# Finding the first batch's attention maxima inside the experts' blocks, on one set of banks

## What is computed

```
x = x + L0_attn_a(layernorm(x))   # 16 heads of 64, softmax
x = x + L0_ffn(layernorm(x))      # 8 experts, each takes the 64 best of 256 tokens
x = x + L0_attn_b(layernorm(x))   # causal, 16 heads of 8, slope bias m * (k - q)
x = x + L0_ffn(layernorm(x))      # the same experts again
x = x + L1_attn_a(layernorm(x))   # causal, 16 heads of 8, rotated q and k
...
```

```
top_p, top_idx = jax.lax.top_k(probs_et, cap)
h = gelu(einsum('BElC,ECH->BElH', xin, w1))
y = einsum('BElH,EHC->BElC', h, w2) * top_p[..., None]
out = zeros.at[b_idx, top_idx].add(y)
```

## Time and profile before

| | us |
|---|---|
| median of 3 runs | 2353.46 |
| the runs | 2351.25 to 2359.56 |
| the profiled execution, its time | 2350.0 |
| its span, first to last instruction | 2348.3 |
| busy in the span: TensorE, VectorE | 2052.1, 1544.7 |
| busy in the span: ScalarE, POOL | 1199.0, 825.0 |
| mean granted clock of TensorE | 0.932 of full |

### The profile page before, as it was taken

The page is one execution under the profiler, slowest core; times in us unless marked ns, Lnnn a source line. Parts: engine busy times, 40 slices in busy tenths (PEclk is TensorE's granted clock), DMA queues, the critical chain, the costliest instruction groups (busy, mean ns, idle before and its releaser), DMA issues. The chain is left out here.

```text
span 2348.3 us, 52692 instructions
## 1 busy us (share of the span) xinstructions
PE 2052.1 (87%) x20735; PEld 1381.5 (59%) x20735; DVE 1544.7 (66%) x2742; ACT 1199.0 (51%) x2044; POOL 825.0 (35%) x1272
## 2 busy tenths in 40 slices
PE   6999999999959997998689989997599985479996
PEld 3666666666648995555578966664345543335553
DVE  5777777777743435666354447774688875768884
ACT  3444444444343324665623326655477776447774
POOL 4444444444423432332144414441233322433330
PEclk9999999999969998999789989998699997769998
DMA  5000000000000022444000214441244420134441
GB/s 167 1 1 1 1 1 1 1 1 1 1 6 2 14 46 70 113 113 99 2 4 1 55 29 113 113 112 32 70 100 115 113 61 1 42 80 107 113 109 46
DMA packets 142787, 120.97 MB, mean 52 GB/s; under 512 B 11808, under 2 KB 127408, under 8 KB 142548
## 3 DMA queue, kind: packets, MB, share of 16 engines
q1 hardware_dynamic: 142548, 117.64, 21.1%
HBM read 63.48 MB, written 54.12 MB: 50 GB/s over the span
## 5 line engine op out<-in xcount | busy, mean ns | idle before, releaser
L906 DVE TENSOR_REDUCE l_group_mx<-maxima 128x4 f32<-128x1024 f32 x248 | 304.0, 1226 | 69.0 <-PE maxima L699 67.5
L834 ACT ACTIVATE l_group_pr<-scores 128x1024 f32<-128x1024 f32 x256 | 261.5, 1021 | 71.7 <-PE scores L720 69.1
L2171 POOL TENSOR_TENSOR l_wide_tiles_sum<-l_wide_pr 128x256 f32<-128x256 f32 x256 | 180.7, 727 | 212.4 <-ACT l_wide_pr L2114 212.4
L2142 DVE RECIPROCAL l_wide_rc<-bank 128x256 f32<-128x256 f32 x128 | 223.8, 1749 | 8.4 <-PE bank L2075 7.9
L2114 ACT ACTIVATE l_wide_pr<-scores 128x512 f32<-128x512 f32 x256 | 139.1, 595 | 163.1 <-PE scores L2058 163.1
L2126 DVE TENSOR_REDUCE l_wide_mx<-maxima 128x2 f32<-128x512 f32 x248 | 159.4, 685 | 52.6 <-PE maxima L2038 52.0
L906 DVE TENSOR_REDUCE l_slope_mx<-maxima 128x6 f32<-128x768 f32 x124 | 118.9, 959 | 74.2 <-PE maxima L706 72.7
L2104 ACT ACTIVATE l_wide_qk<-bank 128x512 f32<-128x512 f32 x128 | 76.4, 597 | 175.2 <-PE bank L2025 175.2
L906 DVE TENSOR_REDUCE l_rope_mx<-maxima 128x6 f32<-128x768 f32 x124 | 118.8, 958 | 56.3 <-PE maxima L706 55.4
L834 ACT ACTIVATE l_slope_pr<-scores 128x768 f32<-128x768 f32 x128 | 103.5, 809 | 87.0 <-PE scores L727 86.8
L834 ACT ACTIVATE l_rope_pr<-scores 128x768 f32<-128x768 f32 x128 | 103.7, 811 | 77.0 <-PE scores L727 76.8
(11 more groups left out here) (468 smaller groups left out, 4853.5 us busy)
## 6 DMA issues: line engine op xcount, KB each, us to landing
l_group_st<-stack_dram SPq DMA_DIRECT2D x64, 384.0 KB, 5.5
l_slope_st<-stack_dram SPq DMA_DIRECT2D x32, 384.0 KB, 5.6
l_rope_st<-stack_dram SPq DMA_DIRECT2D x32, 384.0 KB, 5.5
stack_dram<-l_group_parts SPq DMA_DIRECT2D x64, 192.0 KB, 2.3
stack_dram<-l_group_parts SPq DMA_DIRECT2D x64, 128.0 KB, 1.9
stack_dram<-l_slope_parts SPq DMA_DIRECT2D x32, 192.0 KB, 2.4
stack_dram<-l_rope_parts SPq DMA_DIRECT2D x32, 192.0 KB, 2.3
stack_dram<-l_slope_parts SPq DMA_DIRECT2D x32, 128.0 KB, 2.3
```

What stands on the lines that cost most here:

```text
L834: act.activation(pr[:, i % AHEAD, :, 0:keys], Tp[:, :, 0:keys], ACT.Exp).then_inc(s["exps"], 1)
L906: dve.tensor_reduce(mx[:, b % 2, :, :, i], max_bank(i, b)[:, :, 0:BLOCKS * keys].rearrange("p z (a k) -> p z a k", k=keys), AX.X, ALU.max, ...
L2142: own.done(dve.reciprocal(rc[:], Ob[i % 2][:, S:2 * S]))
L2171: pool.tensor_tensor(tiles_sum[:, i % 2, z, :], pr[:, i % 2, z, 0:S], pr[:, i % 2, z, S:2 * S], ALU.add).then_inc(s["added"], 1)
```

## The change

For slope and rope the list `FIRST` gets all the work on the first batch's maxima: 8 max, turnmax, join, split, shift and spread. The table of hosts gets slots for them in steps 6 and 7 and `expert_schedule` offers "host" there. In the block these maxima go to the scatter's two banks, now one tensor called `values`; each waits for the reduction of the one before. Turnmax goes to the same banks. In the attention itself the maxima 1 and 3 of batch 1 now alternate to `Tp`, which no score uses yet. The tiles `mx`, `mrest`, `cols` and `rows` are allocated earlier.

```diff
+for _kind in ("slope", "rope"):
+    FIRST[_kind]["pe"] += [("max", _i, 0) for _i in range(PAIRS)] + [("turnmax", 0, 0)]
+    FIRST[_kind]["dve"] += [("max", _i, 0) for _i in range(PAIRS)] + [("join", 0, 0), ("turnmax", 0, 0)]
+    FIRST[_kind]["pool"] += [("split", 0, 0)]
+    FIRST[_kind]["sp"] += [("shift", 0, 0), ("spread", 0, 0)]
...
+for _kind in EXPERT_HOST:
+    for _at in [(6, _slot) for _slot in range(3, 9)] + [(7, 3), (7, 4), (7, 8)]:
+        EXPERT_HOST[_kind]["pe"][_at] = "first"
+    for _at in [(6, _slot) for _slot in range(4, 9)] + [(7, 0), (7, 4), (7, 5), (7, 6), (7, 8)]:
+        EXPERT_HOST[_kind]["dve"][_at] = "first"
+    EXPERT_HOST[_kind]["pool"][7, 6] = "first"
...
         def max_bank(i, b):
-            return Tp if b == 0 and i % 2 else Sp
+            if causal and b == 0:
+                return K.Op
+            return Tp if takes_turns(i, b) else Sp
+
+        def takes_turns(i, b):
+
+            return i in (1, 3) and b == 1 if causal else i % 2 and b == 0
+
+        def settled(i, b):
+
+            turns = (b == 1 and 1 <= i <= 4) if causal else b == 0
+            return PAIRS * b + i - (1 if turns else 0)
...
-                wait(pe, s["maxed"], PAIRS * b + i - (1 if b == 0 else 0))
+                wait(pe, s["maxed"], settled(i, b))
...
                     if b == 0:
-                        pe.wait_ge(s["maxed"], PAIRS)
+                        pe.wait_ge(s["maxed"], PAIRS + 4 if causal else PAIRS)
...
-            done = [fill[what, b] for what, i, b in firsts("pe")[:len(firsts("pe")) - len(todo["pe"])]]
+            done = firsts("pe")[:len(firsts("pe")) - len(todo["pe"])]
+            wait(pe, s["maxed"], sum(1 for what, i, b in done if what == "max"))
+            done = [fill[what, b] for what, i, b in done if what != "max"]
...
-        if 2 <= n <= 5:
+        if 2 <= n <= 7:
             pieces.append(("host", slot))
...
-            following.first("sp", sp, 4 * HOSTED)
+            following.first("sp", sp, 4 * HOSTED + 2)
```

More of the change, by code:

```diff
@@ L438 @@
 }
-FIRST["group"] = FIRST["slope"]
+FIRST["group"] = {_engine: list(_pieces) for _engine, _pieces in FIRST["slope"].items()}
 for _kind in FIRST:
@@ L513, in narrow_attention @@
         va = K.va
-        mx = mrest = cols = rows = pr = rc = ot = att = att_t = None
+        pr = rc = ot = att = att_t = None
+        mx = sb("mx", [P, 2, 2, BLOCKS, PAIRS])
+        mrest = sb("mrest", [P, 2, NT, PAIRS])
+        cols = sb("cols", [P, 2, NT, 3, 2, PAIRS], BF16)
+        rows = sb("rows", [48, 2, S], BF16)
         first_norm = sb("first_norm", [P, 6, HOSTED * NT])
@@ L549, in bank_of @@
         def bank_of(what, b):
-            early = causal and b < HOSTED and what in ("norm", "qk", "swapped", "v")
+            early = causal and (b < HOSTED and what in ("norm", "qk", "swapped", "v") or b == 0 and what == "turnmax")
             return (Ob if early else Mb)[fill[what, b][0]]
@@ L1101, in run @@
         def run():
-            nonlocal mx, mrest, cols, rows, pr, rc, ot, att, att_t
+            nonlocal pr, rc, ot, att, att_t
             assert not any(todo.values())
[L1104 to L1107, removed]
             pr = sb("pr", [P, AHEAD, 2, 2 * S])
@@ L2209, in program @@
         banks = [K.Sp[:, 0, :], K.Sp[:, 1, :], K.Tp[:, 0, :], K.Tp[:, 1, :]]
-        banks += [ctx.enter_context(nc.psum_tensor(f"bank{n}", [P, 512], F32)) for n in range(4, 8)]
+        K.Op = ctx.enter_context(nc.psum_tensor("values", [P, 2, 512], F32))
+        banks += [K.Op[:, 0, :], K.Op[:, 1, :]]
+        banks += [ctx.enter_context(nc.psum_tensor(f"bank{n}", [P, 512], F32)) for n in range(6, 8)]
         K.rows_dram = nc.dram_tensor("rows_dram", [16, S], BF16).ap()
```

## The result

The changed kernel takes 2378.28 us (median of 4 runs, 2369.06 to 2385.48), the kernel before 2352.36 beside it; the ratio is 1.0097, 95% interval 1.0074 to 1.012. In a second comparison it took 2379.65 (6 runs) against 2352.4 (29 runs), ratio 1.0117 (1.0087 to 1.0147). So the change costs 25 to 27 us. Forecast were 2364.8, range 2356 to 2373: the direction was right, but of the loss less than half was foreseen (11.3 us).

What follows compares the result with a forecast made beforehand. TensorE was taken to bound the experts' blocks, the stack's transfer loop the attention's pace. Cost 2 x 11.6 = 23.2 us, less gains 7.2 + 4.7 = 11.9, gave +11.3, hence 2364.8 us; range 2356 to 2373.

Steps and rivals of the forecast that it cites:

- the gain at the start: Attention start: earlier first scores, limited by batch 2's stack, save 7.2 us in slope and 4.7 in rope, 11.9 together.
- The waits: Experts' units 6 and 7: TensorE's maxima wait for VectorE's reductions, three times 0.95 and three times 1.85, 8.4 us per block.
- The free case: Rival for the experts' blocks: VectorE is ready in time, no waits; net -5.5 us, 2348; chance 0.10.
- the halved waits: Rival for the experts' blocks: sooner reductions or overlapping work about halve the waits; net +3 us, 2356; chance 0.12.
- Cost 1: Experts' blocks, TensorE: eight maxima's matmuls at 0.38 us each add 3.0 us per block.
- Cost 3: Experts' last unit: maxima's transposes fit the 0.78 us gap before the last scatter; only their copy costs, 0.2 us per block.
- The waits cost the clock: Rival for the experts' blocks: 1.85 us waits lower TensorE's clock, up to 10 us in all, 2375; chance 0.14.
- the prediction's own sign of being wrong: Experts' blocks: a granted clock below 1.0 there was listed among the observations that would show the forecast wrong.
- the next bound: Attention start: batch 2's stack is late next; just in time in slope, a 1.6 to 2.6 us wait in rope.
- The scale: Whole kernel: the profiled execution was 3.5 us below the median, so 2361.3 on the profile's scale became 2364.8.
- the first rival: Experts' blocks: interleaving is free, no waits; net -5.5 us, 2348; chance 0.10.

Runs made afterwards that it cites:

- the filled waits: Changed kernel, with TensorE repeating the next expert's first product ahead of each of the six waiting maxima per block: 2372.6 us, ratio 1.0082 to the kernel before.
- the version without waits: Changed kernel, with VectorE's reductions ahead of its copies in units 6 and 7: 2356.82 and 2360.74 us in two sets, both ratio 1.0016 to before.
- the third batch's early stack: Changed kernel with VectorE reducing first, and batch 2's norm, qk, split and stack moved into the experts' blocks: 2350.29, again 2342.9 us.
- the third batch alone: Batch 2's preparation in the experts' blocks, but batch 0's maxima at the attention's start as in the kernel before: 2358.31 us, ratio 1.0007 to before.

## Why the prediction was wrong in size

The net loss is 25.0 us by the means and was forecast at 11.3. The steps that failed are the clock, put at nothing in the sum, the gain at the start, taken over whole to the end, and the price of a maximum.

- **The waits** (8.4 us per block): right. 8.1 measured from start to start, six of them, each where it was worked out and, to about 0.1 us, as long. The free case and the halved waits are refuted by the same rows. The order on VectorE's queue makes them: once it is turned round, 21 us go, the clock's share with them.
- **Cost 1, a maximum at 0.38 us**: mis-sized. Measured 0.58. The pitch was taken where the maximum stands in the attention, and counted only up to the next start; the pieces before and behind it also grow by 0.10 each. 8 x 2 x 0.2 = 3.2 us.
- **Cost 3, the last unit**: turnmax does not fall into the gap before the scatter. It comes at the end of the last "down", where the gap only begins, and the wait for its copy follows: 0.4 us instead of 0.2.
- **"The waits cost the clock"**, held as a rival at 0.14 and at nothing in the sum: this step failed in its mechanism. The argument against it was that TensorE works without a gap between the waits. That did not help; the clock fell inside units 6 and 7 of every block in both profiled executions, each time behind a wait of 1.74 us. It costs 1.6 to 2.8 us per block, which the filled waits give back. A clock below 1.0 inside the block was the prediction's own sign of being wrong. The rival's 2375 was nearer than the forecast, but in part by luck: its price, up to 5 us per block, was two to three times the measured one, and the rest of the gap came from the start.
- **The gain at the start** (7.2 and 4.7): 5.8 and 4.1 at batch 2's first maximum in the profile. The stack is the next bound, as said; in rope it was issued 3.66 us sooner (3.65 expected), in slope 4.51 (4.87 expected). But at the end only part of the 11.9 is left: 6 to 7 us by the means of the version without waits, and 5 to 7 in the changed kernel, if its blocks cost 29.7 to 31.8 us more as in the two profiles. The forecast took an earlier start for an earlier end; this is the largest single miss, 5 to 7 us. In rope the head start runs into the stack and then into the lower clock, which the third batch's early stack confirms; where slope's part goes was not shown.
- **The scale.** The profiled execution after is 10 us under the later median of its kind, that before 4 under its mean of 2354.0. Of the 26 us the profiles pair to only 19; the second profile adds 2 us in the blocks and has attentions 9.0 us longer than before at a lower clock. Which waits bring it there was not parted.

In sum, for the first profile: 29.8 spent instead of 23.2 (maxima 3.2, clock 3.2, last unit 0.4, waits 0.5 less, 0.3 open), 9.9 won instead of 11.9. By the means: 25.0 is what the blocks cost, 29.7 to 31.8, less the 5 to 7 that are left of the gain.

One slip in its working changes nothing: 894.6 + 0.65 + 0.4 + 2.0 is 897.65 and not 897.8, and the same 0.15 stands in rope's 1386.7. Reckoned from the last scatter, the first scores came 0.5 later than worked out in slope and 0.4 sooner in rope.

The rule of the Trainium skill named in the prediction (page "Perfetto Trace Analysis", section "Optimizing Tensor Performance": rotate through PSUM banks) pointed at a cost that this trace has, the 7.8 us of idle time per block, but the banks need not be rotated here: one set is enough once the reader of the bank comes first in its queue. Without the waits the change was still not faster than before (3.8 us over), and the first rival's gain of 5.5 did not come. The page's other rule, in section "Identifying Performance Opportunities", that interleaving stretches with different limits may pay, is borne out here only together with the early stack (7.0 us under the kernel before).

## What to carry to other kernels

When work is hosted in a block that one engine bounds, ask where its partner step stands on the other engine's queue, not how idle that engine is: one copy ahead of a reduction made 7.8 us of waits per block. Price a foreign piece by what the block grows, neighbours included. A wait of TensorE can have a second price in the clock behind it, so look at the granted clock there too. And a start that is moved forward is worth only what the next late transfer leaves: find that transfer, and move its preparation too.

## What the runs showed that was not expected

- TensorE was busy without a gap but for waits of 0.85 and 1.74 us, and still its granted clock fell to 0.50, for 3 to 7 us, behind a wait of 1.74: at one or two of the three in every block, and not always the same. With the same waits filled it stayed at 1.00.
- Eight bf16 matmuls of a maximum cost 0.28 us themselves and 0.30 at their edges among f32 matmuls at full clock.
- The two halves need each other: the maxima in the blocks without waits take 3.8 us more than the kernel before, the third batch alone 2.8 more (both within 1 to 6 us, and barely clear of noise), both together 7.0 less.
- Executions of one kernel differ by 15 us and more (2345.15 to 2368.94 for the kernel before), and the slower ones have mostly the lower mean clock (0.935 to 0.924). One profiled execution can be 10 us from the median of its kernel, as much as the effect that was looked for.
